# List blocks one place sooner, their one-hots in three parts, and ScalarE's copy of the turned neighbour first

## The reference, cut to what matters

```python
h  = relu(layernorm(x))
x1 = x + relu(concat(h, segsum(h[src], dst), segsum(edge_attr, dst)) @ L0_W.T + L0_b)
g  = relu(layernorm(x1))
g1 = relu(segsum(g[src], dst) / max(deg, 1) @ W1_l + b1 + g @ W1_r)
out = x1 + relu(segsum(g1[src], dst) / max(deg, 1) @ W2_l + b2 + g1 @ W2_r)
```

## Time and profile before

| | us |
|---|---|
| median of three executions | 1666.36 |
| the profiled execution, its own time | 1668.61 |
| its span | 1666.9 |
| round 0, 1, 2 in the span, about | 788 to 1102, 1102 to 1383, 1383 to 1654 |

### The profile page before, as it was taken

The page is one execution under the profiler, slowest core; times in us unless marked ns, Lnnn a source line. Parts: engine busy times, 40 slices in busy tenths (PEclk is TensorE's granted clock), DMA queues, the critical chain, the costliest instruction groups (busy, mean ns, idle before and its releaser), DMA issues.

```text
span 1666.9 us, 36687 instructions
## 1 busy us (share of the span) xinstructions
PE 1452.7 (87%) x12361; PEld 1289.8 (77%) x12362; DVE 876.9 (53%) x2037; ACT 462.4 (28%) x1421; POOL 631.5 (38%) x648
## 2 busy tenths in 40 slices
PE   5674999999888888888999999999999889998785
PEld 5563999888888788887887777778887778887564
DVE  4756888777776676676244554442333332232222
ACT  0191022344456565565222222211111010000000
POOL 2311000000000000000707777634777775577774
PEclk9696999999999999999999999999999999999897
DMA  5005676777877777776644555555555466565452
GB/s 148 22 15 143 187 199 202 205 216 209 230 211 211 216 224 205 212 225 206 219 132 145 158 164 156 145 173 161 172 177 156 155 155 204 167 194 159 151 149 64
DMA packets 278468, 285.18 MB, mean 171 GB/s; under 512 B 17045, under 2 KB 247648, under 8 KB 278416
## 3 DMA queue, kind: packets, MB, share of 16 engines
q1 hardware_dynamic: 231221, 204.41, 40.1%
q0 software_dynamic: 24144, 69.23, 15.2%
q10 hardware_dynamic: 23051, 10.89, 2.3%
HBM read 239.47 MB, written 45.00 MB: 171 GB/s over the span
## 4 chain that ended last, share of the span: by engine, by line
PE 57%; POOL 19%; issue 11%; DVE 4%; ACT 3%; DMA 1%; DVEq 0%; POOLq 0%; ACTq 0%
PE edge_banks L975 22%; PE edge_banks L1011 19%; POOL shared L800 18%; PE banks L957 10%; PE banks L1029 2%; PE edge_banks L972 2%; ACT own L1144 1%; PE edge_banks L1039 1%; PE edge_banks L1018 1%; DVE shared L1538 0%; DVE shared L1535 0%; ACT g_even L1141 0%; DMA shared<-g_rows,list_src 0%; PE banks L1023 0%; PE banks L907 0%
## 5 line engine op out<-in xcount | busy, mean ns | idle before, releaser
L800 POOL DMA_INDIRECT shared<-g_rows,list_src x555 | 571.9, 1031 | 286.7 <-issue 170.6
L1011 PE MATMUL edge_banks<-g_even,shared 128*128 128x257 f16 (+1 forms) x3822 | 447.6, 274 | 5.6 <-DMA shared<-counts 4.5
L1011 PEld LDWEIGHTS edge_banks<-g_even,shared 128*128 128x128 fp8e3 x3822 | 374.8, 98 | 65.4 <-issue 5.0
L975 PE MATMUL edge_banks<-shared 128*128 128x128 f32 x3136 | 408.7, 285 | 0.0
L975 PEld LDWEIGHTS edge_banks<-shared 128*128 128x128 f32 x3136 | 379.7, 198 | 1.0
L780 POOL DMA_DIRECT2D counts<-shared x39 | 20.8, 534 | 612.7 <-ACT shared L1181 612.7
L1181 ACT ACTIVATE shared<-banks 128x392 uint16<-128x392 f32 x312 | 153.9, 494 | 344.8 <-PE banks L957 338.9
L957 PE MATMUL banks<-shared 128*128 128x196 f16 x1764 | 191.0, 254 | 52.3 <-issue 41.3
L1011 PE MATMUL edge_banks<-shared 128*128 128x256 f16 x1911 | 226.3, 273 | 1.5 <-DVE own L1516 1.0
L1535 DVE SCALAR_TENSOR_TENSOR shared<-edge_banks,shared,own 128x128 f32<-128x128 f32 x98 | 34.4, 351 | 359.4 <-PE edge_banks L1011 280.6
L957 PEld LDWEIGHTS banks<-shared 128*128 128x128 f16 x1764 | 166.8, 143 | 64.3 <-issue 50.7
(11 more groups left out here) (267 smaller groups left out, 1084.2 us busy)
## 6 DMA issues: line engine op xcount, KB each, us to landing
shared<-in_edge_attr SPq DMA_DIRECT2D x195, 512.0 KB, 4.1
shared<-counts SPq DMA_DIRECT2D x117, 784.0 KB
counts<-shared POOLq DMA_DIRECT2D x39, 784.0 KB, 4.9
shared<-g_rows,list_src POOLq DMA_INDIRECT x555
g_rows<-g_even SPq DMA_DIRECT2D x1, 3136.0 KB, 15.1
g_rows<-shared ACTq DMA_DIRECT2D x49, 64.0 KB
g_rows<-g_even ACTq DMA_DIRECT2D x49, 64.0 KB
out<-x_sb ACTq DMA_DIRECT2D x12, 192.0 KB
```

Of the source, the lines that this page charges most:

```text
L800: pool.indirect_dma_start(ring_g[k % 2][:, t, 0:2 * D], None, g_rows[r], bass.IndirectOffsetOnAxis(ap=list_src[:, at + t:at + t + 1], axis ...
L975: mm = pe.matmul(edge_wide[bank][:, :, bass.ds(col[j // PAIR], SPREAD)], ring[:, bank * GROUP_TILES + j, :], hot_dst[u][:, k * GROUP_TILES ...
L1011: mm = pe.matmul(acc[s][:, 0:wide], stream8[slot][:, order[h], :], G[r % 2][:, order[h], 0:wide], start=h == 0, stop=h == BLOCKS - 1, skip ...
```

## The change

`FIRST` is 8: positions 0 to 7 are unrolled, 8 to 47 are the loop and 48 is written out behind it. Listed blocks stand at 11, 15, ... 47; `turns_none` holds at 7, 11, ... 47. Position 48 is a dense block, which turns 46 and 47, so the first block of the next round turns only 48; it starts when 46 rows are done and waits ahead of its last three matmuls. `list_dst` is float32 in another place. VectorE writes the one-hots tile by tile with `tensor_scalar`, a third of them (6, 6 and 6 or 7) at the end of its work on each of the three dense blocks ahead of the listed one; the semaphore `list_hot` rises with the last tile. ScalarE's `high` is cut in two, and at a position with `turns_none` the copy of the neighbour's transpose stands ahead of the block's own square root and h. GpSimd's waits follow the new positions, and so do the stores. The core of the diff (TensorE's wait for `list_hot` at a listed block is not in it: it is as before):

```diff
-        FIRST = 9
+        FIRST = 8
-        PER_SLOT = [3, 12, 12, 12]
+        PER_SLOT = [13, 12, 12, 2]
         def is_listed(i):
-            return i >= FIRST and i % 4 == 0
+            return i >= FIRST and (i - FIRST) % 4 == 3
         def turns_none(i):
-            return i >= FIRST - 1 and i % 4 == 0
+            return i >= FIRST - 1 and (i - FIRST) % 4 == 3
         def to_turn(i, r):
             if i == 0:
-                return (2, 1) if r > 0 else ()
+                return (1,) if r > 0 else ()
...
+            one(FIRST + LOOP, LOOPS - 1)          # whole_round, behind the loop; SyncE too
...
# GpSimd
-                        done = r * BLOCKS + FIRST + 4 * k if k >= 2 else r * BLOCKS + 4 * k - 4
+                        done = r * BLOCKS + FIRST + 4 * k if k >= 2 else r * BLOCKS + 4 * k - 1
...
# TensorE, first block of a round
+                        last = BLOCKS - 3 if new else NEAR_END
-                            pe.wait_ge(R["g_done"], r * BLOCKS)
+                            pe.wait_ge(R["g_done"], r * BLOCKS - 1)
...
# ScalarE
                         if r == 0:
                             copy_edge(after(i, it), n + 1, 1 - s)
+                        if turns_none(i):
+                            turned(1)
+                        if r == 0:
                             act.wait_ge(R["aggr"], n + 1)
...
                         if turns_none(i):
                             high(1)
                             store(2)
+                            turned(0)
                             high(0)
...
# VectorE
-                        if i >= FIRST and i % 4 == 2:
-                            lists = bass.ds(it * MOST + (0 if i - FIRST >= 4 else LOOPS * MOST), MOST)
-                            dve.tensor_tensor(list_hot_u8, iota16[:, 0:P].unsqueeze(1).broadcast_to([P, MOST, P]),
-                                              list_dst[:, lists].unsqueeze(2).broadcast_to([P, MOST, P]), ALU.is_equal).then_inc(R["list_hot"], 1)
+                        if FIRST <= i < FIRST + LOOP and not is_listed(i):
+                            k, part = (i - FIRST) // 4, (i - FIRST) % 4
+                            for t in range(part * MOST // 3, (part + 1) * MOST // 3):
+                                if t < LIST_TILES[k]:
+                                    col = bass.ds(it * MOST + (t + (0 if k else LOOPS * MOST)), 1)
+                                    ins = dve.tensor_scalar(list_hot_u8[:, t, :], iota16[:, 0:P], list_dst[:, col], None, ALU.is_equal)
+                            if part == 2:
+                                ins.then_inc(R["list_hot"], 1)
```

More of the change, by code:

```diff
@@ L131, in message_passing @@
         row_sum = sb("row_sum", [P, NDUO])
[L132 to L135, removed]
+        norm_t = sb("norm_t", [P, 5 * BLOCKS])
+        mean_var = norm_t[:, 0:2 * BLOCKS].rearrange("p (b k) -> p b k", k=2)
+        std, scale, shift = (norm_t[:, k * BLOCKS:(k + 1) * BLOCKS] for k in (2, 3, 4))
+        list_dst = norm_t[:, 0:NLIST]
         list_src = sb("list_src", [P, NLIST], I32)
@@ L203, in message_passing @@
         list_hot_u8 = list_hot_u8.rearrange("p (t d) -> p t d", d=P)
-        list_dst = place(25008, NLIST // 2).bitcast(F16)
-        assert r1 + MOST * P // 4 <= 24496 and 25008 + NLIST // 2 <= SHARED and NLIST % 2 == 0
+        assert r1 + MOST * P // 4 <= 24496 and NLIST <= 5 * BLOCKS
         tile_rows = place(0, TCOLS).bitcast(I32).rearrange("p (b e) -> p b e", e=P)
@@ L714, in rounds @@
                                 one(i, it)
+                        one(FIRST + LOOP, LOOPS - 1)
                     else:
@@ L1058, in one @@
                         edge_sum()
-                        sums(turn_at, NEAR_END)
+                        sums(turn_at, last)
                         if 1 in turns:
                             dense(1)
-                        for h in range(NEAR_END, BLOCKS):
+                        for h in range(last, BLOCKS):
                             if new:
@@ L1206, in one, with turned, high @@
                         bs = block_at(place_of(i, it))
+                        def turned(back):
+                            o = (s + back) % 2
+                            act.wait_ge(R["turned"], n + 3 - back)
+                            act.activation(hT_blk[:, o, :], turn_ps[o], ACT.Copy).then_inc(R["hT_done"], 1)
+                        def high(back):
+                            o = (s + back) % 2
+                            at = block_at(before(i, it, back) if back else place_of(i, it))
+                            act.wait_ge(R["g_up"], n + 1 - back)
+                            act.activation(G[(r + 1) % 2][:, at, 0:D].rearrange("p a f -> p (a f)"), g_ps[o][:, 0:D], ACT.Copy,
+                                           scale=up[:, r + 1:r + 2]).then_inc(R["g_high"], 1)
                         if r == 0:
                             copy_edge(after(i, it), n + 1, 1 - s)
+                        if turns_none(i):
+                            turned(1)
+                        if r == 0:
                             act.wait_ge(R["aggr"], n + 1)
@@ L1214, in one @@
                                            bias=tiny[:, s, 2:3], scale=tiny[:, s, 1:2]).then_inc(R["h_done"], 1)
[L1216 to L1223, removed]
                         def store(back):
@@ L1240, in rounds @@
                     whole_round(act, one)
[L1241 to L1244, removed]
+                    b = place_of(FIRST + LOOP, LOOPS - 1)
+                    act.wait_ge(R["g_done"], (r + 1) * BLOCKS + 2)
+                    act.dma_start(g_rows[r + 1][b * P:(b + 1) * P], G[(r + 1) % 2][:, b, 0:2 * D]).then_inc(g_stored[r + 1], 16)
                 def send(done, b, n):
@@ L1250, in send @@
                     act.dma_start(rows.rearrange("(b p) f -> p b f", p=P), blocks).then_inc(R["out_stored"], 16)
-                for done, b, n in ((3, 0, 3), (6, 3, 3), (9, 6, 2), (9, DENSE - 1, 1)):
+                for done, b, n in ((3, 0, 3), (6, 3, 3), (7, 6, 1), (8, DENSE - 1, 1)):
                     send(done, b, n)
@@ L1255, in of_loop @@
                     send(it * LOOP + (FIRST + 3), place_of(FIRST, it), 3)
-                    if not last:
+                    if last:
+                        act.wait_ge(R["fin"], it * LOOP + (FIRST + 4))
+                        act.dma_start(out[(BLOCKS - 1) * P:N], x_sb[0:TAIL, BLOCKS - 1, :]).then_inc(R["out_stored"], 16)
+                    else:
                         send(it * LOOP + (FIRST + 4), place_of(FIRST + 3, it), 1)
@@ L1261, in rounds @@
                     of_loop(it, False)
[L1262 to L1263 removed]
                 of_loop(LOOPS - 1, True)
+                send(BLOCKS, place_of(FIRST + LOOP, LOOPS - 1), 1)
                 act.wait_ge(R["out_stored"], 16 * OUT_STORES)
@@ L1528, in one @@
                         if i == 0 and r > 0:
-                            for ago in (2, 1):
-                                split(r - 1, before(0, 0, ago), n - ago, (s + ago) % 2)
+                            split(r - 1, before(0, 0, 1), n - 1, 1 - s)
                         dve.wait_ge(R["summed"], n + 5)
```

8 lines of the change are left out of this document (4 added, 4 removed).

## The result

| | before | after |
|---|---|---|
| median of four executions, us | 1667.05 (1664.75 to 1671.2) | 1723.7 (1719.83 to 1726.09) |
| span of the profiled execution | 1666.9 | 1723.6 |
| mean granted clock | 0.950 | 0.948 |

The kernel became slower: ratio 1.0335, 95% interval 1.0305 to 1.0365. 1728 was forecast.

A forecast was written before the change was run, and what follows sets the result against it. PE was taken as the busiest engine, waiting for ScalarE in round 0 and gathers in rounds 1 and 2. Terms of +43, +20 and -1 gave +62: 1668.6 to 1731, forecast 1728 as median, range 1705 to 1750.

The forecast's parts named there:

- The listed block's wait: At each listed block TensorE waits for VectorE's one-hots: 4.5, 3.0 and 2.9 us in rounds 0, 1, 2.
- (a)+(b): Block ahead of the list: VectorE sees the sum and does its whole work, 3.27, 1.82, 1.74 us by round.
- Part (c): Last third of the one-hots: 6 or 7 tiles at 0.17 us, 1.1 us, plus 0.1 for end and semaphore.
- The clock behind the wait: Matmuls behind each list's wait run at the lower clock level: excess 1.8 us in round 0, 1.2 in rounds 1 and 2.
- rival A: Behind the list waits PE stays at the high clock level: +62 - 42 = +20, 1687 us; chance 0.16.
- ScalarE's copy first: Round 0: both PE waits for ScalarE go, 18.6 us, and one slow stretch, 1.3; the late square root hides.
- The gathers: Rounds 1 and 2: gather waits of 15.9 and 32.2 us go, with slow stretches of 5.9 and 9.9.
- Rival B: At the last thirds, tiles cost 0.24 us and stand for gathers up to 0.94 us: 1757 us; chance 0.13.
- Position alone: In each round, moving the listed blocks one position earlier is worth nothing, as the blocks are the same.
- Sum: Rounds 0, 1, 2 of the profiled execution: +43, +20, -1, together +62 us.
- C: At the 30 lists the wait is far shorter; at 1.9 us per list -27, 1639 us; chance 0.05.
- D: At the lists, tiles at 0.08 us and no clock excess: 87 - 84 = +3, 1669 us; chance 0.04.

The follow-up runs named there:

- one tile left: The changed kernel with its tiles divided 9, 8 or 9, and 1, a single tile behind the last dense block; 1689.12 us, ratio 1.0156.
- the run at the old positions: The halves with the list blocks back at 12, 16, ... 48, ScalarE's new order kept; 1613.09 us, ratio 0.9689.
- The halves: The changed kernel with tiles written in two halves behind the first two of the three dense blocks; 1612.61 us, 0.9698 (first run 2167.89 us, 0.9966).
- the tiles alone: The kernel before with only the one-hots written tile by tile, two blocks ahead of the list; 1637.58 us, 0.9837 (first run 2182.12 us, 1.0025).
- all of it left behind the block ahead: The changed kernel with one tensor_tensor for all tiles behind the block right ahead of the list; 2338.42 us, ratio 1.0839.

## Why the prediction was right, step by step

- *The listed block's wait*: predicted 4.5, 3.0, 2.9 us; measured 4.72, 3.31, 3.23. The part (a)+(b), VectorE's own work, was right almost to the hundredth: 3.26 us at the list shown against 3.27, 1.83 at the second list of round 1 and 1.73 at the sixth of round 2 against 1.82 and 1.74. Part (c) was undersized in both its pieces. Six tiles start to start take (1.27 - 0.28) / 5 = 0.20 us each, not 0.17, inside the bounds; in the row of seven at 1226.03 (1.73 us) some stood longer. And from the last tile's start to TensorE's first matmul it is 0.28 + 0.24 us, so the end and the hand-over add 0.32 us to the 0.20 and not 0.1. Over 30 lists the waits are 9 us more than summed.
- *The clock behind the wait*: predicted 1.8, 1.2, 1.2 us a list, 42 in all. Measured, by the start of the 61st TensorE instruction behind the list's first one against the same at a list at 2.4 GHz: 1.3 to 2.8 us a list in round 0, 18.7 in all; 6.1 us in round 1, at three lists; 11.6 us in round 2, at seven lists with 1.65 each: 36. The term was 6 us too large, all of it in round 1, where seven of ten lists kept the high level. PE in round 1, second list, then fourth:

```profile
1228.00 4.21 PE L1041 MATMUL edge_banks<-shared 128*128 128x256 f16 x19 [3.64 <-DVE shared L1579]
```

```profile
1280.09 2.25 PE L1041 MATMUL edge_banks<-shared 128*128 128x256 f16 x19 [3.37 <-DVE shared L1579]
```

  After 3.64 us of standing still the 19 matmuls take twice their time, the 1.2 GHz level; after 3.37 us they do not. Seven lists running, with waits of 3.2 to 3.4 us, kept 2.4 GHz. In round 2 seven of ten lists with waits of 3.1 to 3.6 us were slow, in round 0 all ten with 4.6 to 4.8. A longer wait did not mean a slow list: 3.37 us kept the high level here, and 2.19 us lost it in the kernel with one tile left. So rival A (the clock holds) held at seven lists in round 1 and at three in round 2. "As many slow lists as waits" was wrong: 20 of 30. So was "PEclk falls in all three rounds": it is 0.99, 0.97 and 0.95 before and 0.93, 0.98 and 0.96 after, since the slow stretches behind the gather waits went in rounds 1 and 2.
- *ScalarE's copy first*: both waits of round 0 went, as said, and no new wait on the square root came. What went was worth more than its 18.6 us. From the first of the ten matmuls ahead of the older `turn` to the first behind the `dense`, before and then after:

```profile
873.81 1.28 PE L1011 MATMUL edge_banks<-g_even,shared 128*128 128x257 f16 x10
...
878.96 2.29 PE L1011 MATMUL edge_banks<-g_even,shared 128*128 128x257 f16 x19
```

```profile
869.18 1.28 PE L1013 MATMUL edge_banks<-g_even,shared 128*128 128x257 f16 x10
...
871.96 2.29 PE L1013 MATMUL edge_banks<-g_even,shared 128*128 128x257 f16 x19
```

  That is 5.15 us against 2.78. Over the eleven places the starts give 23.7 us where the view of waits, which counts from a matmul's modelled end, gave 18.6.
- *The gathers*: their waits went in rounds 1 and 2, as the longer interval of TensorE left POOL its lead, and no gather exceeds 1.06 us. Rival B (tiles stand for gathers) holds only in small amounts: 407 of the 555 tiles overlap a gather and last 0.305 us on the average, the other 148 last 0.278; the longest is 0.52 us against a median of 0.28. The Trainium skill, SBUF — State Buffer, section "Who interferes with whom", names `tensor_scalar` as an operation that may take the shared port pair, in a two-port mode; whoever comes second then waits for the whole of the other's instruction. The trace shows no such full wait: a tile that met a gather of 0.94 us lost at most 0.24 us. Whether the tiles ran in a two-port mode no run here shows.
- *Position alone*: nothing, as said, shown by the run at the old positions.
- *Sum*: +43, +20, -1 predicted for the rounds, +39, +18, +2 measured. The mechanism and each term's sign were right, but the nearness of the total is in part luck. The waits were 9 us larger than their term, the clock 6 smaller, and what went was 89 us (112.6 + 36.4 less the 59.6 of the rounds) and not 84, the difference lying in round 0. That makes +60 for the rounds; the stage ahead of them was 2.5 us shorter in the profiled execution after (its first sum starts at 790.92 against 793.38), and so the spans differ by 57 where 62 was forecast.
- *The range*: 1705 to 1750 doesn't follow from what is named beside it. Two thirds of the clock term take off 14 us, which is 1714, and a tile at 0.24 adds 14, which is 1742. The measured 1723.7 lies inside these too.

Rivals C and D fell by the waits themselves: about 3.2 to 4.7 us a list is over the 2.8 us at which the sign would have turned.

## What to carry to other kernels

When an engine that must not stand still consumes what another one writes, the last piece belongs behind an earlier block, not at the end of the producer's work on the block right ahead: here the same instructions cost 3.4% or gain 3.0%, by that alone. Price such a wait as the whole work of the producer on that block plus the piece, and expect a clock penalty behind it that may or may not come. A removed wait is paid out only as far as the next resource allows: on the kernel before, ScalarE's order took away 17 us of waits in round 0 and shortened it by 13, as gathers came late there instead.

## What the runs showed of the hardware that was not expected

**The same kernel can take 30% longer on another chip, with TensorE idle for no wait in the profile.** In two jobs the kernel before took 2176.54 and 2161.22 us; on other chips it took 1662 to 1667. Every kernel in those jobs was longer by some 500 us or more. The halves in the first such job: busy shares, where the chain goes, and two matmuls of a round.

```profile
PE 1572.4 (73%) x12361; PEld 1315.4 (61%) x12362; DVE 910.8 (42%) x2562; ACT 462.7 (21%) x1421; POOL 585.2 (27%) x648
...
PE 64%; issue 20%; another core or an unknown queue 8%; DVE 4%; ACT 2%; DMA 1%; DVEq 0%; ACTq 0%; POOL 0%; POOLq 0%
```

```profile
PE edge_banks L1013 <- issue: 292.9, 245, 3.1
```

```profile
1300.52 0.37 PE L1013 MATMUL edge_banks<-shared 128*128 128x256 f16 x1 [1.54 <-issue]
1301.23 0.39 PE L1013 MATMUL edge_banks<-shared 128*128 128x256 f16 x1 [0.34 <-issue]
```

The busy times of VectorE, ScalarE and POOL are those of an undisturbed chip, but TensorE gets one matmul in 0.7 us in stretches where it starts one each 0.11 us elsewhere. No data wait stands before them. Nearly all of the extra time lies in the rounds: the first gather starts at 789.0 us, against 783.5 in the same kernel on an undisturbed chip. That the instructions came late is inferred from this. The queues that the page calls "instruction" moved the same 27 and 26 packets in both, in 0.1% of the engines' time or less, so a slower loading of them is not seen, and the cause stays open. Ratios from such jobs are no measure of a change: the halves gave 0.9966 there and 0.9698 elsewhere, and the tiles alone 1.0025 against 0.9837.

**Equal waits, unequal clock.** A stand of 3.1 to 3.4 us was followed by 1.2 GHz at some lists and by 2.4 GHz at others of the same shape, seven of the latter in a row. With one tile left, a stand of 2.19 us in round 1 was followed by 1.2 GHz at seven lists of ten, and one of 2.1 to 2.3 us in round 2 at none of nine. The length of the wait alone does not tell what follows. What a fall costs is steadier: 1.65 us at most of the slow lists, 2.9 at most.

**What holds a gather.** One `tensor_tensor` of 2.69 us with both inputs in SBUF stretched gathers to 3.4 us and one over half the tiles to 2.2. The same work in `tensor_scalar` tiles of 0.28 us never stretched one beyond 1.09. With the long instruction right ahead of the list (all of it left behind the block ahead) no gather was longer than 1.02 us: none was under way during any of the 30.
